# A second pass of a graph kernel: a rare refinement written out straight instead of in nested loops

## The reference

```python
q = X @ W1.T @ W2.T
k = X @ W3.T
probs = jax.nn.softmax(q @ k.T / TAU, axis=-1)
idx = jnp.argsort(-probs, axis=-1)
sp = jnp.take_along_axis(probs, idx, axis=-1)
cs = jnp.cumsum(sp, axis=-1)
keep_sorted = cs - sp < TOP_P
mask = jnp.zeros(probs.shape, dtype=bool).at[rows, idx].set(keep_sorted)
A = probs * mask
A = A / jnp.maximum(A.sum(-1, keepdims=True), 1e-12)
```

## Time and profile before

| what | value |
|---|---|
| median of 3 runs | 6814.19 us |
| profiled execution, and its span | 6809.27 us, 6807.5 us |
| VectorE busy | 5323.6 us, 78% of the span |
| TensorE matmuls busy | 4464.3 us, 66% |
| ScalarE busy | 2196.1 us, 32% |
| HBM traffic over the span | 79 GB/s |

### The profile page before, as it was taken

One profiled execution on the slowest core, in us unless ns is written; L12 is line 12 of the kernel. 1 busy time (PEld: TensorE's weight loads), 2 busy tenths in 40 slices (PEclk: granted clock), 3 DMA queues, 4 the chain that ended last, 5 costly groups with the idle time before them and its releaser, 6 DMA issues. The chain is left out here.

```text
span 6807.5 us, 80595 instructions
## 1 busy us (share of the span) xinstructions
PE 4464.3 (66%) x27812; PEld 3192.8 (47%) x27812; DVE 5323.6 (78%) x13061; ACT 2196.1 (32%) x3353; POOL 325.5 (5%) x170
## 2 busy tenths in 40 slices
PE   6995788888664364523455488853537888855983
PEld 2442477777553354422455477743511222214982
DVE  5885688888168888887888889988458999995875
ACT  2332676666111111111122244321222222213542
POOL 0000000000200000000000000000000220120000
PEclk9997898998897787866778799976769999987996
DMA  7561000000131121111111022210203333322850
GB/s 197 199 204 58 1 2 2 2 2 2 61 129 72 60 101 78 77 44 45 61 52 71 32 91 81 94 56 16 32 16 126 105 107 111 107 64 105 299 206 15
DMA packets 177843, 541.57 MB, mean 80 GB/s; under 512 B 20203, under 2 KB 62302, under 8 KB 177302
## 3 DMA queue, kind: packets, MB, share of 16 engines
q1 hardware_dynamic: 172246, 531.90, 22.5%
q0 software_dynamic: 5120, 3.97, 0.3%
HBM read 524.17 MB, written 11.56 MB: 79 GB/s over the span
## 5 line engine op out<-in xcount | busy, mean ns | idle before, releaser
L679 PE MATMUL ps<-ident,arena 125*125 125x125 f32 x3200 | 540.6, 302 | 1213.0 <-DVEq L1185 1213.0
L679 PEld LDWEIGHTS ps<-ident,arena 125*125 125x125 f32 x3200 | 470.4, 215 | 1252.9 <-DVEq L1185 1252.8
L711 PE MATMUL ps<-arena 125*125 125x129 f32 x6400 | 822.2, 287 | 323.2 <-DMA arena<-in_adj_tiles 315.9
L1487 DVE SCALAR_TENSOR_TENSOR arena<-arena,pair 125x1000 f32<-125x1000 f32 x800 | 939.3, 1257 | 69.7 <-ACT arena L1450 69.7
L793 ACT ACTIVATE turned<-ps 125x500 f32<-125x500 f32 x800 | 466.5, 585 | 1620.3 <-PE ps L679 1619.5
L711 PEld LDWEIGHTS ps<-arena 125*125 125x125 f32 x6400 | 770.5, 196 | 394.6 <-DMA arena<-in_adj_tiles 310.9
L687 PE MATMUL ps<-arena,turned 125*125 125x129 f32 x6400 | 912.9, 290 | 5.2 <-ACT turned L793 4.8
L1505 PE MATMUL ps<-arena 125*64 125x500 f32 x3200 | 762.5, 599 | 195.1 <-DVE arena L1487 195.1
L687 PEld LDWEIGHTS ps<-arena,turned 125*125 125x125 f32 x6400 | 838.4, 202 | 16.8 <-ACT turned L793 9.4
L1138 DVE SCALAR_TENSOR_TENSOR arena<-arena,wt 125x5000 f32<-125x5000 f32 x80 | 434.1, 5427 | 184.0 <-issue 184.0
L1505 PEld LDWEIGHTS ps<-arena 125*64 125x64 f32 x3200 | 196.9, 137 | 757.7 <-DVE arena L1487 529.8
(11 more groups left out here) (349 smaller groups left out, 6197.9 us busy)
## 6 DMA issues: line engine op xcount, KB each, us to landing
arena<-in_adj_wide SPq DMA_DIRECT2D x400, 500.0 KB, 4.5
arena<-in_adj_tiles SPq DMA_DIRECT2D x400, 488.3 KB
arena<-in_adj_wide SPq DMA_DIRECT2D x100, 1000.0 KB, 4.7
x_saved<-arena SPq DMA_DIRECT2D x2, 2240.0 KB
arena<-x_saved SPq DMA_DIRECT2D x2, 2240.0 KB
arena<-att_saved SPq DMA_DIRECT2D x1, 2257.5 KB
arena<-in_x SPq DMA_DIRECT2D x1, 2240.0 KB
arena<-in_h SPq DMA_DIRECT2D x1, 2240.0 KB
```

Of the source, the lines that this page charges most:

```text
L679: mm = pe.transpose(banks_turn[:, g % 2, c * P:(c + 1) * P], work[b % depth][:, j:j + P], ident[0:P, 0:P])
L711: mm = pe.matmul(acc_spread, ring[:, j * P:(j + 1) * P], values[:, j, :], start=(j == 0), stop=False)
L1487: v.scalar_tensor_tensor(out=weight(m).rearrange("p (g w) -> p g w", g=2), in0=rows(ERB + h * N + r * PASS, PASS).rearrange("p (g w) -> p ...
```

## The change

The two outer loops around `refine` are replaced: `refine` is called once without a test, because the branch at L1170 has just found the number to be 3; the number is then loaded and tested, and a second copy of `refine` stands under that test; the number is loaded and tested a third time, and a loop of ten rounds with a test and a third copy stands under that. Twelve refinements stay the most that are possible. Within `refine` the loops of three and four bisections are written out.

```diff
--- before.py
+++ after.py
@@ -64,7 +64,7 @@
 TINY = 1e-37
 BISECTIONS = 3
 CANDIDATE_BISECTIONS = 4
-REFINE_ROUNDS = (4, 3)
+REFINE_ROUNDS = 12
 LIGHT = 0.55
 SPREADS = (5, 3, [4] * 8 + [0, 3, 3] + [1, 1, 2, 1] * 6 + [2, 2, 0, 0, 0])
 
@@ -1072,14 +1072,14 @@
                     def refine(w, cand):
 
 
-                        with v.Fori(0, BISECTIONS):
+                        for _ in range(BISECTIONS):
                             bisect(w, dump, goal)
                         v.tensor_copy(above_hi, base)
                         v.tensor_tensor(rest, goal, base, ALU.subtract)
                         v.drain()
                         v.memset(base, 0.0)
                         candidates_up_to_hi(w, cand)
-                        with v.Fori(0, CANDIDATE_BISECTIONS):
+                        for _ in range(CANDIDATE_BISECTIONS):
                             bisect(cand, windows, rest)
                         least_in_bracket(cand)
                         lower_hi(cand)
@@ -1172,10 +1172,13 @@
                             jump.branch_hint(early)
                         with on_vector(opened):
                             mass_above(cand, windows, hi, base)
-                            with v.Fori(0, REFINE_ROUNDS[0]):
-                                second = worst()
-                                with v.If(second > 2):
-                                    with v.Fori(0, REFINE_ROUNDS[1]):
+                            refine(w, cand)
+                            second = worst()
+                            with v.If(second > 2):
+                                refine(w, cand)
+                                third_time = worst()
+                                with v.If(third_time > 2):
+                                    with v.Fori(0, REFINE_ROUNDS - 2):
                                         more = worst()
                                         with v.If(more > 2):
                                             refine(w, cand)
```

## The result

The changed kernel takes 6703.99 us, the median of 4 runs (6701.96 to 6706.88), against 6815.29 us for the kernel before (4 runs, 6812.01 to 6816.69). The ratio is 0.9838, with a 95% interval of 0.9821 to 0.9855. The forecast was 6719 us, with a range of 6686 to 6764.

What follows compares the result with a forecast made beforehand. VectorE was taken to bound the attention steps. Entry 26, loops 32, exit 40 and 9, less 8 for jumps, made 99 us, taken as 95: 6719 us from the median, 8 in 10 within 6686 to 6764; own range 6690 to 6765.

Steps and rivals of the forecast that it cites:

- Entry: From last group sum to first bisection in 16 opened blocks: idle falls from 1.70 to 0.08 us each, 26 us saved.
- Loops: Bisection loops of 19 refinements: turns fall from 0.36 and loop ends from 0.23 to 0.08 us, 32 us saved.
- Exit: L908 to L1138 in 16 opened blocks: 4.4 us each, 40 us saved; 9 us more for hinted lines still held.
- Jumps in the first attention: Jumps to the plain part: shifted line boundaries make more of them long, 8 us lost, bounds -5 and +16 us.
- the 7 on the edge: First-attention steps that might, in the changed layout, lack a line boundary between hint and branch, beyond 7 certain ones.
- Stalls of wrong hints stay: Inside refinements of the seven hinted opened blocks: stalls, 3.2 us in the mean beyond normal, remain unchanged.
- The slower rival: Hints fail over 699 or 762 instructions; 57 plain blocks pay a fetch each, 151 us, giving 6862 us; chance 0.07.
- The exit finds its line: Rival: more lines are held, so all 16 exits take 1.24 us; 141 us saved, 6673 us; chance 0.10.
- The gain is hidden: Rival: TensorE is as late as VectorE, so the gain is given back, 6810 us; chance 0.05.
- rounding down: The terms' sum of 99 us was taken as 95 us, for the small crossings.
- new misses: Plain blocks of the second attention: one or two of 24 jumps might miss, up to 26 us in the range.

## Why the prediction was right, and where not

The profiled executions are 6809.27 and 6705.36 us, 103.9 apart, the medians 111.3. The second attention gives 110.7 us and the first 0.6. The part ahead of the first attention took 735.6 us before and 742.3 after, with nothing changed in it; in the ten other kernels it is 736.5 to 741.5 us. So of the two profiled executions the one before lies below all others there and the one after above them, and the 111 us are the change's.

- *Entry, forecast 26 us*: 27.3 us have become 1.3 us over 16 blocks. Exact. The three second refinements also begin 0.5 us earlier each, which I had left out, 1.4 us.
- *Loops, 32 us*: the turns fell from 0.36 to 0.08 us and the loop ends from 0.23 to 0.07. The idle times hold all of the 32 us: 27.1 in the turns, 2.6 in the end of the first loop (L1077) and 3.1 in that of the second (L1043, 5.9 to 2.8 us). Replaced alone, on top of the rest of the change, the loops are worth 6739.11 - 6703.99 = 35 us, 13 of them in the first attention's jumps.
- *Exit, 40 and 9 us*: measured 54.8. The total is near and its make-up isn't. I charged 4.4 us to each. Seven hinted blocks found their line held, 1.25 to 1.30 us each; this I gave 40%. The nine others cost 47.4 us, 5.3 in the mean. The term that was mis-sized is the price of a miss: I took the mean of the seven stalls, 3.2 us, for all, where it is two prices, 2.2 to 2.6 and 4.9 to 6.1 us, and the DMA share goes with one or the other.
- *Jumps in the first attention, -8 us*: mis-sized too. 53.5 us before, 53.2 after, 7 long gaps each. The 7 that were certain came, none of the 7 on the edge. With the outer loops alone 13 were long.
- *Stalls of wrong hints stay*: 24.4 us in seven blocks before, 27.3 us in six after.
- *The slower rival*: refuted by the trace after (33 jumps over 699 instructions take at most 1.25 us, 24 over 762 at most 1.24), and sized by the version without hints: +146 us in these jumps, where I had reckoned 151, and +128 us for the kernel, since the stalls of wrong hints go.
- *The exit finds its line*: half true, in the seven. A second hint made it true in 14 of 16, and the time then was 6681.60 us; my 6673 us for it counted all.
- *The gain is hidden*: TensorE's wait at L679 for VectorE fell, from 1213 to 1070 us in all; VectorE was still waited for.

The saving is 111 us and not 95. The 16 us between are 8 of the first attention, 6 of the exits, 1.4 of the second refinements, 1 of the loops and 4 of rounding down, less 3 for the longer stalls, which leaves 1 us over. The near hit of the exits is in part luck: seven lines held gave 13 us more than was carried for them, and dearer misses took back 8. The forecast's own range does not add up at its slow end: exits at 13 us saved, jumps at -16 and 26 us of new misses leave 29 us of saving, 6785 us and not 6765.

Three runs show what hints do: without them all 80 jumps wait for an instruction packet and no refinement stalls; moved earlier, no jump of the first attention is long; taken from blocks 9 to 11, the stalls of these go. Each of the six stalls in the kernel after has an instruction packet in it that lands 1.4 to 1.6 us before the stall ends. That a hint does this by redirecting the fetch at a line boundary, in place of the next line, is the reading that fits all three and is not seen by itself. That lines hold 128 instructions is an inference that placed all 7 long gaps of the kernel before; that about four are held is a weaker one, from a hinted line that is still there after the refinement's own lines and from the loops that start to fetch when they grow. Why block 36 alone shows no stall with a wrong hint here, when it has one of 5.3 us in the versions with an exit hint, and why the second hint missed in blocks 0 and 2, stays open.

The Trainium skill, "Runtime: NRT & Kernel Launch", section "Instruction fetch mechanics", draws from its two blocks of 256 instructions that unrolling is the better form. For the change as a whole the times agree. For its half they don't: the bisections alone, written out inside loops that spin without working, made the kernel 24 us slower.

## What to carry to other kernels

Count what a rare path costs when it is over: a loop bound that is "enough" is paid in rounds that only test, 1.24 us each here, and lowering it alone gave 62 us. Write out a body only after the loops around it are gone, and read instruction packets and long gaps named "issue" together. Where a long jump stays, give it a hint with a line boundary between hint and branch, and leave it off blocks that mostly take the other side once their exit has a hint of its own; without that one it made no difference here (6701.11 against 6703.99 us).

## What was not expected of the hardware

- The same jump costs 3.5 to 3.8 us or 6.1 to 7.3 us with the DMA engines at share 0.01 or 0.33; the 8192 byte packet it waits for starts later and takes no longer.
- A loop of testing rounds can cost 46.36 us for five rounds, with 13 instruction packets, against 6.9 us in other blocks of the same code (a single execution).
- A hint placed a whole plain part ahead, with other branches between, still works: 0 of 40 gaps over 1.34 us.
